# Outputs of the first expert layer turned through memory and VectorE, second layer eight blocks behind, pairs of blocks per step

## The chip, the cores and the metric

The kernel runs on one core of a Trainium2 chip. The metric is the device time of one execution in microseconds (us). The kernel before has a median of 285.72 us over 3 runs (285.41 to 286.38).

## What is computed

`x` is [4, 512, 256], 2048 tokens of 256 features, all in float32. With `xn = layernorm(x)` the result is `x + A(xn) + F(xn)`.

- `A` is a recurrent block: `h = rmsnorm(xn)`; `a = sigmoid(h @ w_a + bias)`, `i = sigmoid(h @ w_i)`, `v = h @ w_v`; a scan over time of `s = a*s + sqrt(1 - a*a)*i*v`; `x1 = xn + s @ out_proj`; then a gated feed-forward with 1024 hidden features: `x1 + (silu(g) * u) @ w_down` with `g, u = split(rmsnorm(x1) @ w_gate_up)`.
- `F` is a mixture of 8 experts, each token in its two best: `y = sum over its 2 experts of p * (relu(xn @ w_fc[e])**2 @ w_proj[e])`, the `p` being the softmax of the two router logits.

## The kernel before

**Precision.** Products are of float32 split into a high part (`_hi`, float32r) and a low rest (`_lo`), three matmuls each: hi*hi, hi*lo, lo*hi. Whatever feeds a matmul must thus be split first: ScalarE copies it to `_hi`, VectorE subtracts to `_lo`.

**Stages.** Up to about 60 us the rows are normalised, the router and the recurrence run, and GpSimd scatters every token's row (and its weight and home row) into `xs_dram`, sorted by expert: 39 blocks of 128 rows, each of one expert. The feed-forward of the recurrent block runs in 32 steps `d` (batch `d // 8`, 128 hidden features `d % 8`): TensorE makes `gate_up(d, 0)` and `gate_up(d, 1)` (six products of 512 columns each, the second in two halves), ScalarE `gate(d)` (silu, L870), VectorE `up(d)` (L1234), ScalarE and VectorE `split_gu(d)` (L890, L1239), and TensorE a step later `down(d - 1)` (twelve products of 256 columns).

**Expert blocks** run inside steps 11 to 24, two or three per step (`THREE`), one more after steps 11 and 17 (`PROJECT`: the output projection of batches 2 and 3, L503) and 13 and 20 (`TURN`: the turn of `h2`, L516). For block i:
- SP loads a pair of blocks from `xs_dram` (L350: for each of 4 groups of 32 columns and each half k, one DMA in pieces of 32 columns, so that what 32 partitions hold are 32x32 tiles); VectorE turns them (`block_turn`, L1304), ScalarE writes `xgT_hi` (`block_in`, L900), VectorE `xgT_lo` (L1311).
- TensorE: first layer `FC` (six products of 256 columns), ScalarE `block_relu` (L922), VectorE `block_square` (L1316) into `act_e`.
- TensorE turns `act_e` by two products with the identity into PSUM bank `T2` (L669); ScalarE `block_middle` writes `aT_hi` (L916), VectorE `aT_lo` (L1320).
- TensorE: second layer `PJ` (six products), ScalarE `block_y` scales by the weight (L909), GpSimd scatters the rows to `y_dram` (L1565).

The order is written out by hand for each engine, and each engine works its list strictly in order, with semaphore waits. TensorE's list has, per block i of a step (v is its place in the step): `expert_in(i)` = PJ of i - 2; for v = 0 `gate_up(d, 0)`, for v = 1 the second half of `gate_up(d, 1)` and half of `down(d - 1)`; `expert_out(i)` = turns of block i - 1, then FC of block i; for v = 0 the first half of `gate_up(d, 1)`, for v = 1 the other half of `down(d - 1)`. VectorE's and ScalarE's lists before are:

```python
# VectorE, block i of step d                 # ScalarE
block_turn(i + 1)                            if v == 0: split_gu(d - 1)
if v == 0: split_gu(d - 1)                   if i >= 2: block_y(i - 2)
if v == 1: up(d)                             if v == 0: gate(d)
if i >= 1: block_middle(i - 1)               if i >= 1: block_middle(i - 1)
block_square(i)                              block_relu(i)
block_in(i + 1)                              block_in(i + 1)
```

`cumulate` and `recur` of batch 3 (scans, L1126, L1131) stand in VectorE's list in steps 14 and 15, after the block's own work, and `take_down` adds a batch's down projection to `Y` (L1262). After the last block SP loads the expert rows back in the tokens' order (`sums`, L402), VectorE adds them in steps 27 to 30 (`add_sum`, L1269), and SP stores the output.

Of the kernel before, what the change touches and what calls it, by code (L numbers as in the profile page):

```python
# [36 lines left out]
def recurrent_moe_block(nc, x, pre_norm_w, w_a, w_i, w_v, out_proj_w, decay_bias, ffn_norm_w,  # L37
# [25 lines left out]
    xs_slot = xs_dram.rearrange("(n p) d -> p n d", p=P)  # L63

# [4 lines left out]
    with ExitStack() as ctx:  # L69
# [129 lines left out]
        xr = [small(f"xr{u}", [P, K, P]) for u in range(2)]  # L199
        xgT = [(small(f"xgT{u}_hi", [P, K, P], F32R), small(f"xgT{u}_lo", [P, K, P], F32R)) for u in range(2)]  # L200
        act_e = [small(f"act_e{u}", [P, D]) for u in range(2)]
        aT = [(small(f"aT{u}_hi", [P, K, P], F32R), small(f"aT{u}_lo", [P, K, P], F32R)) for u in range(2)]
# [3 lines left out]
        xq = [put(f"xq{u}", [P, 2, P // Q, K, Q], F32, X_at + 2 * D * 4 * u) for u in range(XQ)]  # L206
# [37 lines left out]
        xq_loaded, of_slot_loaded = [sem(f"xq_loaded{u}") for u in range(XQ)], [sem(f"of_slot_loaded{h}") for h in range(2)]  # L244
# [3 lines left out]
        t2_done, a_hi, a_split = sem("t2_done"), sem("a_hi"), sem("a_split")  # L248
# [18 lines left out]
        for w, halved in ((w_fc, Wfc), (w_proj, Wpj)):  # L267
            for e in (0, 2, 4, 6):
                pieces.append((w[e:e + 2].rearrange("e (k p) n -> p (e k) n", p=P),
                               [h[:, e:e + 2].rearrange("p e k n -> p (e k) n") for h in halved]))  # L270
        ALL = len(pieces)
# [4 lines left out]
        T2, FC, PJ = 3, 6, 7  # L276
        DOWN = 4

# [8 lines left out]
        LAST = 24  # L287

        THREE = (12, 14, 16, 18, 19, 22, 24)
# [6 lines left out]
        ADD_X = {12: 0, 18: 1, 23: 3}  # L296
# [17 lines left out]

        def stored(i):

            return y_stored[i % YB], 16 * (i // YB + 1)

        def gu_bank(d):
# [5 lines left out]
            return 0 if d <= LAST else 2 * ((d - LAST - 1) % 2)  # L325
# [26 lines left out]
        OF_SLOT = (slice(0, 8), slice(8, 2 * NP))  # L352

        def load_of_slot(eng, part):
            eng.dma_start(of_slot[:, OF_SLOT[part], :],
                          xs_slot[:, OF_SLOT[part], WEIGHT:ROW]).then_inc(of_slot_loaded[part], 16)

        @block.sync
        def _(sp):
# [3 lines left out]
            def load_piece(n):  # L363
                sp.dma_start(pieces[n][1][2], pieces[n][0]).then_inc(w_loaded[n], 16)
# [26 lines left out]
            for n in range(NP):  # L391
                if n >= XQ:
                    sp.wait_ge(turned, 2 * (n - XQ) + 2)
                load_pair(sp, n, range(0 if n else P // Q // 2, P // Q))
                if n == 1:
                    load_of_slot(sp, 1)
# [16 lines left out]
        def _(pe):  # L413
# [111 lines left out]
            def gate_up(d, side, part=None):  # L525

                b, m = divmod(d, M)
                if side == 0 and part in (None, 0):
# [10 lines left out]
                    if d == LAST + 2:  # L539
                        pe.wait_ge(a_split, NB)  # L540
# [37 lines left out]
            def down(d, js=range(J)):  # L578
# [4 lines left out]
                if b == B - 1 and m == 0 and js[-1] == J - 1:  # L583
                    pe.wait_ge(act_ready, NB)
# [72 lines left out]
            sets = [[pe.alloc_register(f"expert{s}_{v}") for v in range(SETS)] for s in range(2)]  # L657
            expert = {}

            def load_experts(i):  # L660
                n = min(SETS, NB - i)
                regs = sets[i // SETS % 2][:n]
# [4 lines left out]
            def block_transpose(bank, src, done):  # L667
                for k in range(K):
                    last = nc.tensor.transpose(ps[:, bank, k * P:(k + 1) * P], src[:, k * P:(k + 1) * P], ident[:, :])  # L669
                last.then_inc(done, 1)  # L670

            def layer(bank, lhs, w, v, done):
# [967 lines left out]
```

## Time and profile before

| what | value |
|---|---|
| median of 3 runs | 285.72 us |
| the profiled execution | 284.51 us |
| its span, first to last instruction | 282.7 us |
| TensorE busy, of the span | 269.5 us (95%) |
| VectorE, ScalarE, GpSimd busy | 206.8, 165.7, 114.3 us |
| granted TensorE clock | 1.00 of full speed (2.4 GHz) |
| share of TensorE in the chain that ended last | 75%, VectorE 12% |

The profile is of one execution. Busy times of TensorE are modelled at their ends (matmuls are pipelined), so the distance from one start to the next says more than a duration. "Idle before" an instruction is what its engine waited, and the arrow names who ended it.

### The profile page before, as it was taken

What the parts mean: (1) busy time and instruction counts of PE and PEld (TensorE: products, weight loads), DVE (VectorE), ACT (ScalarE), POOL (GpSimd) and SP (SyncE); (2) the same over time, 40 slices, a digit from 0 to 9 for tenths busy, and PEclk for the clock granted to TensorE, in tenths of its full rate; (3) what the DMA queues carried; (4) which work ended last, traced back from release to release, by engine and by line L of the source; (5) the groups of instructions that cost most, each with busy time, mean ns of one, the idle gap of its engine ahead of it and who ended that gap; (6) DMA issues with size and microseconds to landing.
All of it is one profiled execution on the core that took longest, in us unless ns stands there. A gap on an engine that the chain in (4) does not pass through costs nothing.

```text
span 282.7 us, 5334 instructions
## 1 busy us (share of the span) xinstructions
PE 269.5 (95%) x1671; PEld 234.6 (83%) x1671; DVE 206.8 (73%) x422; ACT 165.7 (59%) x361; POOL 114.3 (40%) x136
## 2 busy tenths in 40 slices
PE   5989999999999979999999999999999999999995
PEld 5767778888888868988997889888898888888894
DVE  3899999999577998656698966565657565533994
ACT  3798889967486433467746555475775555532231
POOL 6597015888668820046233332155222242250000
PEclk9999999999999999999999999999999999999999
DMA  7999992239202147429424344239434365119962
GB/s 212 352 389 314 293 330 73 94 109 353 99 20 92 60 94 49 61 51 180 82 64 82 68 90 82 47 43 197 84 69 79 67 96 118 37 39 280 381 230 77
DMA packets 75590, 39.15 MB, mean 138 GB/s; under 512 B 50758, under 2 KB 72268, under 8 KB 75564
## 3 DMA queue, kind: packets, MB, share of 16 engines
q1 hardware_dynamic: 67760, 27.10, 38.4%
q0 software_dynamic: 5520, 11.44, 14.1%
q10 hardware_dynamic: 2284, 0.27, 0.7%
q8 instruction: 15, 0.25, 0.3%
q14 instruction: 11, 0.09, 0.1%
HBM read 22.07 MB, written 16.72 MB: 137 GB/s over the span
## 4 chain that ended last, share of the span: by engine, by line
PE 75%; DVE 12%; ACT 4%; DMA 3%; issue 3%; POOL 2%; SPq 0%; ACTq 0%; DVEq 0%; POOLq 0%
PE ps L415 64%; PE ps L503 4%; PE ps L669 3%; DMA sums<-y_dram 2%; PE ps L516 1%; PE ps L419 1%; PE ps L432 1%; ACT h L849 1%; DVE aT_lo L1320 1%; DVE gu L1234 1%; ACT aT_hi L916 1%; DVE guT_lo L1239 1%; DMA y_dram<-yb,home_u 1%; DVE hT_lo L1100 1%; DVE cum L1126 1%
## 5 line engine op out<-in xcount | busy, mean ns | idle before, releaser
L1565 POOL DMA_INDIRECT y_dram<-yb,home_u x39 | 41.3, 1059 | 91.4 <-ACT yb L909 69.7
L1544 POOL DMA_INDIRECT xs_dram<-rows_x,slot_u x32 | 40.5, 1266 | 11.3 <-issue 10.2
L415 PE MATMUL ps<-h2T_lo,Wgu_hi 128*128 128x512 f32 (+1 forms) x132 | 42.4, 386 | 0.0
L415 PE MATMUL ps<-h2T_hi,Wgu_hi 128*128 128x512 f32 (+1 forms) x132 | 41.0, 391 | 0.0
L1320 DVE TENSOR_TENSOR aT_lo<-ps,aT_hi 128x256 fp32r<-128x256 f32 x39 | 16.5, 423 | 32.9 <-ACT aT_hi L916 32.9
L415 PE MATMUL ps<-h2T_hi,Wgu_lo 128*128 128x512 f32 (+1 forms) x132 | 40.4, 387 | 0.0
L415 PE MATMUL ps<-Wd_hi,guT_hi 128*128 128x256 f32 x128 | 36.6, 286 | 1.8 <-DVE Y L1262 1.6
L870 ACT ACTIVATE gu<-ps 128x512 f32<-128x512 f32 x31 | 18.5, 597 | 31.2 <-PE ps L415 31.2
L415 PE MATMUL ps<-Wd_hi,guT_lo 128*128 128x256 f32 x128 | 36.2, 283 | 0.0
L415 PE MATMUL ps<-Wd_lo,guT_hi 128*128 128x256 f32 x128 | 36.1, 282 | 0.0
L1234 DVE TENSOR_TENSOR gu<-gu,ps 128x512 f32<-128x512 f32 x31 | 21.1, 682 | 18.8 <-PE ps L415 18.8
L909 ACT ACTIVATE yb<-ps,of_slot 128x256 f32<-128x256 f32 x39 | 18.5, 474 | 20.4 <-PE ps L415 20.4
L890 ACT ACTIVATE guT_hi<-gu 128x512 fp32r<-128x512 f32 x31 | 19.5, 628 | 15.6 <-DVE gu L1234 13.1
L415 PEld LDWEIGHTS ps<-h2T_lo,Wgu_hi 128*128 128x128 f32 x132 | 24.5, 188 | 4.9
L415 PEld LDWEIGHTS ps<-h2T_hi,Wgu_lo 128*128 128x128 f32 x132 | 24.5, 188 | 4.7
L415 PEld LDWEIGHTS ps<-Wd_hi,guT_hi 128*128 128x128 f32 x128 | 24.1, 189 | 4.2 <-issue 2.0
L916 ACT ACTIVATE aT_hi<-ps 128x256 fp32r<-128x256 f32 x39 | 14.9, 381 | 20.4 <-PE ps L669 20.4
L415 PEld LDWEIGHTS ps<-Wd_lo,guT_hi 128*128 128x128 f32 x128 | 24.1, 189 | 1.1
L415 PEld LDWEIGHTS ps<-Wd_hi,guT_lo 128*128 128x128 f32 x128 | 24.1, 188 | 0.0
L415 PEld LDWEIGHTS ps<-h2T_hi,Wgu_hi 128*128 128x128 f32 x132 | 21.7, 188 | 1.9
L1239 DVE TENSOR_TENSOR guT_lo<-gu,guT_hi 128x512 fp32r<-128x512 f32 x31 | 20.9, 673 | 3.2 <-ACT guT_hi L890 3.0
L415 PE MATMUL ps<-Wpj_hi,aT_hi 128*128 x78 | 17.8, 309 | 3.1 <-DVE aT_lo L1320 3.1
(175 smaller groups left out, 622.2 us busy)
## 6 DMA issues: line engine op xcount, KB each, us to landing
xs_dram<-blank SPq DMA_DIRECT2D x1, 5160.0 KB, 27.1
xq<-xs_dram SPq DMA_DIRECT2D x156, 32.0 KB, 2.1
sums<-y_dram SPq DMA_DIRECT2D x8, 512.0 KB, 7.7
Wgu_raw<-in_L_attn_w_gate_up_dram SPq DMA_DIRECT2D x4, 512.0 KB, 8.7
Wfc_raw<-in_L_ffn_w_fc_dram SPq DMA_DIRECT2D x4, 512.0 KB, 10.2
Wpj_raw<-in_L_ffn_w_proj_dram SPq DMA_DIRECT2D x4, 512.0 KB, 6.2
rows_x<-in_L_attn_x_dram SPq DMA_DIRECT2D x3, 512.0 KB, 6.6
rows_x<-in_L_attn_x_dram POOLq DMA_DIRECT2D x3, 512.0 KB, 6.1
```

Of the source, the lines that this page charges most:

```text
L415: return nc.tensor.matmul(dst, lhs, rhs, start=start, stop=stop, skip_group_check=group)
L503: last = nc.tensor.matmul(ps[:, aside(b) + side, (j % 2) * D:(j % 2 + 1) * D], dec[b][:, k, j * P:(j + 1) * P], Wo[:, k, :], start=k == 0, ...
L669: last = nc.tensor.transpose(ps[:, bank, k * P:(k + 1) * P], src[:, k * P:(k + 1) * P], ident[:, :])
L870: A.activation(gu[d % 2][:, :], ps[:, gu_bank(d), :], ACT.Silu).then_inc(sg_ready, 1)
L890: A.activation(guT[d % 2][0][:, :], gu[d % 2][:, :], ACT.Copy).then_inc(gu_hi, 1)
L909: A.activation(yb[i % YB][:, :], ps[:, PJ, 0:D], ACT.Copy, scale=of_slot[:, i, 0:1]).then_inc(y_ready, 1)
L916: A.activation(aT[i % 2][0][:, :, :].rearrange(flat), ps[:, T2, 0:D], ACT.Copy).then_inc(a_hi, 1)
L1234: V.tensor_tensor(gu[d % 2][:, :], gu[d % 2][:, :], ps[:, gu_bank(d) + 1, :], ALU.mult).then_inc(gu_ready, 1)
L1239: V.tensor_tensor(guT[d % 2][1][:, :], gu[d % 2][:, :], guT[d % 2][0][:, :].bitcast(F32), ALU.subtract).then_inc(gu_split, 1)
L1320: V.tensor_tensor(aT[i % 2][1][:, :, :].rearrange(flat), ps[:, T2, 0:D], aT[i % 2][0][:, :, :].rearrange(flat).bitcast(F32), ALU.subtract) ...
L1544: pool.indirect_dma_start(out=xs_dram, in_=rows_x[:, b, j, :], in_offset=None, out_offset=bass.IndirectOffsetOnAxis(ap=slot_u[:, n:n + 1], ...
L1565: pool.indirect_dma_start(out=y_dram, in_=yb[i % YB][:, :], in_offset=None, out_offset=bass.IndirectOffsetOnAxis(ap=home_u[:, i:i + 1], ax ...
```

## The change

- First-layer outputs are no longer turned by TensorE. SP stores the pair's `act_e` to a new `act_dram` (two DMAs), loads it back in 32-column pieces (four DMAs into `aq`, one per 32 partitions), and VectorE turns it per block (`act_turn`) into `aT_raw`, which lies at the place of `aT_lo`. `block_middle` then reads SBUF and not PSUM.
- The second layer of block i - 8 (`LAG`) runs in front of block i. The first layer ends with step 23 (`LAST`), the last eight second layers run four per step in 24 and 25 (`DRAIN`). `FC` and `PJ` have two PSUM banks each.
- `block_turn`, `block_in`, `block_relu`, `block_square` work on pairs (512 columns), each in every second block.
- The token rows are loaded in pieces of 64 columns, four DMAs a pair for eight; for that `w_fc`'s rows are loaded in another order (16 DMAs for 4). The weights and homes of the slots come in one DMA.
- In VectorE's list the `take_down`s of batch 0 stand in front of `cumulate(2, 1)`.

The core of the diff (comment-free; "..." marks what is left out):

```diff
+    act_dram = nc.dram_tensor("act_dram", [NP, K, 2 * P, P], F32, kind="Internal").ap()
+    act_pair = act_dram.rearrange("n k (a i) c -> n i (k a) c", i=Q)
...
-        LAST = 24
-        THREE = (12, 14, 16, 18, 19, 22, 24)
+        LAST = 23
+        DRAIN = 25
+        LAG = 8
+        THREE = (12, 14, 15, 16, 18, 19, 21, 22, 23)
...
         def load_pair(eng, n, groups):
             for r in groups:
-                mine = xq[n % XQ][r * Q:(r + 1) * Q].rearrange("i v g k c -> i (v g) k c")
-                for k in range(K):
-                    col = k * P + r * Q
-                    eng.dma_start(mine[:, :, k, :], xs_pair[n, :, :, col:col + Q]).then_inc(xq_loaded[n % XQ], 16)
+                eng.dma_start(xq[n % XQ][r * Q:(r + 1) * Q].rearrange("i a k c -> i a (k c)"),
+                              xs_pair[n, :, :, r * K * Q:(r + 1) * K * Q]).then_inc(xq_loaded[n % XQ], 16)
...
+            def store_act(n):
+                sp.wait_ge(act_ready, n + 1)
+                for v in range(2):
+                    sp.dma_start(act_dram[n, :, v * P:(v + 1) * P, :].rearrange("k p c -> p k c"),
+                                 act_e[n % 2][:, v, :].rearrange("p (k c) -> p k c", c=P)).then_inc(act_stored[n % 2], 16)
+
+            def load_act(n):
+                if n >= 2:
+                    sp.wait_ge(a_turned, 2 * n - 2)
+                else:
+                    sp.wait_ge(o_done, 6)
+                sp.wait_ge(act_stored[n % 2], 32 * (n // 2 + 1))
+                for r in range(P // Q):
+                    sp.dma_start(aq[n % 2][r * Q:(r + 1) * Q].rearrange("i k v g c -> i (k v g) c"),
+                                 act_pair[n, :, :, r * Q:(r + 1) * Q]).then_inc(aq_loaded[n % 2], 16)
...
-            for n in range(NP):
-                if n >= XQ:
-                    sp.wait_ge(turned, 2 * (n - XQ) + 2)
-                load_pair(sp, n, range(0 if n else P // Q // 2, P // Q))
+            for n in range(NP + 4):
+                if n < NP:
+                    if n >= XQ:
+                        sp.wait_ge(turned, n - XQ + 1)
+                    load_pair(sp, n, range(0 if n else P // Q // 2, P // Q))
...
+                if n >= 4:
+                    load_act(n - 4)
+                if 3 <= n < NP + 3:
+                    store_act(n - 3)
...
             # TensorE
+            def expert_out(i):
+                if i >= 0:
...
+                    pe.wait_ge(a_split, i + 1)
+                    if i >= 2:
+                        pe.wait_ge(y_ready, i - 1)
+                    layer(PJ[i % 2], 0, aT[i % 2], slice(0, P), Wpj, expert[i], pj_done)
...
+                    for v, i in enumerate(blocks_of(d)):
+                        expert_out(i - LAG)
                         if v == 0:
                             gate_up(d, 0, 0)
                             gate_up(d, 0, 1)
                         if v == 1:
                             gate_up(d, 1, 1)
                             down(d - 1, range(0, 2))
-                        expert_out(i)
+                        expert_in(i)
                         if v == 0:
                             gate_up(d, 1, 0)
                         if v == 1:
                             down(d - 1, range(2, 4))
+                elif d <= DRAIN:
+                    d0, d1, d2, d3 = drained_by(d)
+                    expert_out(d0)
+                    gate_up(d, 0)
+                    expert_out(d1)
+                    gate_up(d, 1)
+                    expert_out(d2)
+                    down(d - 1)
+                    expert_out(d3)
...
             # ScalarE
                     for v, i in enumerate(blocks_of(d)):
+                        block_y(i - LAG - 1)
                         if v == 0:
                             split_gu(d - 1)
...
                             gate(d)
...
+                        if i % 2 == 0:
+                            block_relu(i // 2 - 1)
+                        block_middle(i - LAG + 1)
+                        if i % 2 == 1:
+                            block_in(i // 2 + 1)
...
             # VectorE
+            def act_turn(i):
+                if 0 <= i < NB:
+                    n, v = divmod(i, 2)
+                    dve.wait_ge(aq_loaded[n % 2], 16 * (P // Q) * (n // 2 + 1))
                     if i >= 2:
+                        dve.wait_ge(pj_done, i - 1)
+                    V.transpose(aT[i % 2][2][:, :, :].rearrange("p k (g s) -> p k g s", s=Q),
+                                aq[n % 2][:, :, v, :, :]).then_inc(a_turned, 1)
...
-            cumulate(2, 1)
             take_down(0, 0)
             take_down(0, 1)
+            cumulate(2, 1)
...
                     for v, i in enumerate(blocks_of(d)):
-                        block_turn(i + 1)
+                        act_turn(i - LAG + 1)
...
                         if v == 1:
                             up(d)
-                        if i >= 1:
-                            block_middle(i - 1)
-                        block_square(i)
-                        block_in(i + 1)
+                        if i % 2 == 0:
+                            block_turn(i // 2 + 1)
+                        else:
+                            block_in(i // 2 + 1)
+                        if i % 2 == 0:
+                            block_square(i // 2 - 1)
+                        block_middle(i - LAG + 1)
...
                 if d in PROJECT or d in TURN:
                     i = block_after(d)
+                    act_turn(i - LAG + 1)
                     if d in PROJECT:
                         add_residual(PROJECT[d], 0)
                     if d in TURN:
                         split_h2(TURN[d], range(0, 1))
-                    block_square(i)
-                    block_in(i + 1)
+                    if i % 2 == 0:
+                        block_turn(i // 2 + 1)
+                    else:
+                        block_in(i // 2 + 1)
+                    if i % 2 == 0:
+                        block_square(i // 2 - 1)
+                    block_middle(i - LAG + 1)
                     if d in TURN:
                         split_h2(TURN[d], range(1, 2))
```

## Rows read from the trace of the kernel before

**Rows 1.** Busy time, clock and DMA in the stretch of the expert blocks.
```profile
core 0: us, PE busy (x) PEld busy (x) DVE busy (x) ACT busy (x) POOL busy (x), PEclk, DMA share, GB/s
109.46:251.92 142.46, 139.07 (x949) 125.34 (x950) 93.94 (x214) 82.29 (x213) 47.51 (x46) 1.00 0.44 81
```

**Rows 2.** Waits: who waited for whom: us in total, times, longest.
```profile
PE ps L415 <- DVE aT_lo L1320: 3.1, 7, 0.4
...
PE ps L415 <- DVE Y L1262: 1.6, 1, 1.6
```

**Rows 3.** Pieces of the chain that ended last: start us, us, what.
```profile
139.31 0.44 PE ps L516 x4
...
176.12 1.73 PE ps L503 x8
177.85 0.22 PE ps L669 x2
```

**Rows 4.** Timeline of step 19: start us, us, engine line op out<-in.
```profile
190.19 0.48 PE L415 MATMUL ps<-Wpj_hi,aT_hi 128*128 x2 [0.43 <-DVE aT_lo L1320]
...
190.99 0.62 PE L415 MATMUL ps<-h2T_hi,Wgu_hi 128*128 128x512 f32 x2
...
192.37 0.38 PE L669 MATMUL ps<-ident,act_e 128*128 128x128 f32 x2
...
192.57 0.60 ACT L870 ACTIVATE gu<-ps 128x512 f32<-128x512 f32 x1 [0.91 <-PE ps L415]
...
193.06 0.38 ACT L916 ACTIVATE aT_hi<-ps 128x256 fp32r<-128x256 f32 x1
...
193.47 0.42 DVE L1320 TENSOR_TENSOR aT_lo<-ps,aT_hi 128x256 fp32r<-128x256 f32 x1 [1.57 <-ACT aT_hi L916]
...
194.03 0.48 PE L415 MATMUL ps<-Wpj_hi,aT_hi 128*128 x2
...
195.79 0.69 DVE L1234 TENSOR_TENSOR gu<-gu,ps 128x512 f32<-128x512 f32 x1 [0.74 <-PE ps L415]
...
196.23 0.38 PE L669 MATMUL ps<-ident,act_e 128*128 128x128 f32 x2
...
197.16 0.28 PE L415 MATMUL ps<-Wd_hi,guT_hi 128*128 128x256 f32 x1
```

**Rows 5.** Timeline where the first expert block starts.
```profile
106.83 1.22 DVE L1229 TENSOR_TENSOR Wpj_lo<-Wpj_raw,Wpj_hi 128x1024 fp32r<-128x1024 f32 x1
...
107.97 0.44 DVE L1304 STREAM_TRANSPOSE xr<-xq 128x256 f32<-128x256 f32 x1
...
108.44 0.42 ACT L900 ACTIVATE xgT_hi<-xr 128x256 fp32r<-128x256 f32 x1 [2.55 <-DVE xr L1304]
...
108.76 0.61 ACT L890 ACTIVATE guT_hi<-gu 128x512 fp32r<-128x512 f32 x1
108.89 0.43 DVE L1311 TENSOR_TENSOR xgT_lo<-xr,xgT_hi 128x256 fp32r<-128x256 f32 x1 [0.48 <-ACT xgT_hi L900]
...
109.46 0.51 PE L415 MATMUL ps<-Wfc_hi,xgT_hi 128*128 x2 [0.50 <-DVE xgT_lo L1311]
```

**Rows 6.** Timeline: start of step 14, last second layer, steps 26 to 28.
```profile
139.61 0.48 PE L415 MATMUL ps<-Wpj_hi,aT_hi 128*128 x2
...
250.49 0.28 PE L415 MATMUL ps<-Wd_hi,guT_hi 128*128 128x256 f32 x1
...
251.92 0.62 PE L415 MATMUL ps<-h2T_hi,Wgu_hi 128*128 128x512 f32 x2
...
261.35 1.23 DVE L1269 TENSOR_TENSOR Y<-Y,sums 128x1024 f32<-128x1024 f32 x1 [1.51 <-DMA sums<-y_dram]
...
263.36 0.39 PE L415 MATMUL ps<-Wd_hi,guT_hi 128*128 128x256 f32 x1
```

**Rows 7.** The tile `xq`: its loads by SP (issue, ns min/median/max) and landing.
```profile
L350 SPq DMA_DIRECT2D xq<-xs_dram x156: 302/451/1271, 102.8 to 233.5; - x156
...
DMA to landing us min/median/max: 1.7/2.1/4.7
```

More of the change, by code:

```diff
@@ L198, in recurrent_moe_block, with turned_halves @@
         over = [moe_at]
[L199 to L202, printed above, removed]
+        def turned_halves(name, n):
+            hi = small(name + "_hi", [P, K, n * P], F32R)
+            at = over[0]
+            return hi, small(name + "_lo", [P, K, n * P], F32R), put(name + "_raw", [P, K, n * P], F32, at)
+        xgT = [turned_halves(f"xgT{u}", 2) for u in range(2)]
+        aT = [turned_halves(f"aT{u}", 1) for u in range(2)]
         yb = [small(f"yb{u}", [P, D]) for u in range(YB)]
@@ L313, in recurrent_moe_block, with drained_by @@
         assert blocks_of(LAST)[-1] == NB - 1
+        def drained_by(d):
+            return range(NB - LAG + 4 * (d - LAST - 1), NB - LAG + 4 * (d - LAST))
+        assert drained_by(DRAIN)[-1] == NB - 1
         def stored(i):
@@ L656, in _ @@
             pe.wait_ge(experts_ready, 1)
-            sets = [[pe.alloc_register(f"expert{s}_{v}") for v in range(SETS)] for s in range(2)]
+            sets = [[pe.alloc_register(f"expert{s}_{v}") for v in range(SETS)] for s in range(4)]
             expert = {}
@@ L665, in load_experts, with layer @@
                     expert[i + v] = pe.snap(reg, min_val=0, max_val=E - 1)
[L667 to L672, printed above, removed]
+            def layer(bank, half, lhs, cols, w, v, done):
                 for n, (l, h) in enumerate(PRODUCTS):
                     for k in range(K):
-                        last = product(ps[:, bank, 0:D], lhs[l][:, k, :], w[h][:, v, k, :],
+                        last = product(ps[:, bank, half * D:(half + 1) * D], lhs[l][:, k, cols], w[h][:, v, k, :],
                                        n + k == 0, n == 2 and k == K - 1)
@@ new lines, in expert_in @@
+                if i % SETS == 0:
+                    load_experts(i)
+                if v == 0:
+                    pe.wait_ge(xg_split, n + 1)
+                    if n >= 2:
+                        pe.wait_ge(act_ready, n - 1)
+                    if n == 0:
+                        pe.wait_ge(we_lo, FFN_ALL + 4 - 3)
+                    if n == 1:
+                        pe.wait_ge(gu_ready, FIRST)
+                layer(FC[n % 2], v, xgT[n % 2], slice(v * P, (v + 1) * P), Wfc, expert[i], fc_done)
@@ L1284, in add_down, with homes @@
                                     ALU.add).then_inc(out_ready, 1)
-            def homes(part):
-                dve.wait_ge(of_slot_loaded[part], 16)
-                mine = OF_SLOT[part]
-                at = of_slot[:, mine, 1]
-                chain.step(V.scalar_tensor_tensor(out=no_home[:, mine], in0=at, scalar=0.0, in1=no_home[:, mine],
+            def homes():
+                dve.wait_ge(of_slot_loaded, 16)
+                at = of_slot[:, :, 1]
+                chain.step(V.scalar_tensor_tensor(out=no_home[:, :], in0=at, scalar=0.0, in1=no_home[:, :],
@@ L1606, in _ @@
                         add_x(ADD_X[d])
-                if (d in PROJECT or d in TURN) and block_after(d) >= 3:
-                    scatter(block_after(d) - 3)
-            for i in range(NB - 3, NB):
+                if (d in PROJECT or d in TURN) and block_after(d) > LAG:
+                    scatter(block_after(d) - LAG - 1)
+            for i in range(NB - LAG - 1, NB):
                 scatter(i)
```

273 lines of the change are left out of this document (135 added, 138 removed).

## The prediction

> **What bounds the kernel now.** I read the windows view first, over the stretch in which the expert blocks run: from the first product of block 0 to the start of step 26 the span has 142.46 us, TensorE (PE) is busy in 139.07 of them, VectorE in 93.94, ScalarE in 82.29, the granted clock is 1.00 of full speed (2.4 GHz) and the DMA engines are busy 0.44 of the time [rows 1]. So PE sets the pace here, and a change pays only in what PE does or waits for. The waits view then says who PE waits for: 1.6 us once for a sum of the down projection (`Y` L1262), and 3.1 us in 7 waits for `aT_lo`, the low half of the turned outputs that the second layer eats [rows 2]. The idle time is counted against modelled ends; by start times each of the 7 costs 0.6. The pieces of the chain give PE's unit prices: 0.22 us for the two turns of a block, 1.73 for half a projection, 0.44 for half an h2 turn [rows 3].
>
> The third reading is one step in the timeline [rows 4], d = 19, since all that follows is built from it. From the start of a second-layer product at 190.19 it takes 0.80 to the first gate product, 1.38 for six products of 512 columns (to 192.37), and 0.93 for the two turns with a first-layer product (196.23 to 197.16), so a layer's six products of 256 columns take 0.71. ScalarE starts `gate` 2.38 after the start of the block, the next instruction 0.49 later (it starts 0.11 before the end of a 0.60 one); VectorE's `aT_lo` takes 0.42, and PE starts 0.14 after it, at 194.03: 3.84 after 190.19, of which PE's own work is 3.8. The present order is thus already at the limit: gate, aT_hi, aT_lo, next block. In the next block `up` starts 1.76 after PE's start.
>
> **The change, part by part.**
> Removed: 39 pairs of turns, 39 x 0.22 = 8.6 us, and the 7 waits of 0.6 = 4.2 us, since they come from a turn that is followed at once by the product that needs it. A layer that comes after 512-column products takes 0.80 and not 0.71, which stays in the own times below. VectorE, which turns the outputs instead, needs 0.44 for 256 columns [rows 5] where PE needs 0.22, but has room. The Trainium skill, "VectorE: DVE Perf Modes" (Rules for kernel authors), speaks against the swap: a full 128x128 turn belongs on TensorE where the result may go to PSUM, as it may here. By that rule the swap would cost up to 39 x (0.44 - 0.22) = 8.6 us where the rows alone give 8.6 us back; the sum below takes the rows, since VectorE has room for the 17 us.
>
> Own time of PE, per block, afterwards. First block of a step (v0): 0.80 + 1.38 + 0.79 + 0.69 = 3.66. Second (v1): 0.80 + 0.69 + 3 x 0.71 = 3.62. Third (v2): 0.80 + 0.71 = 1.51.
>
> Added: the order in which `aT_lo` is made. PE begins block i with the second layer of i - 8, whose `aT_lo` is made by VectorE at the end of its list for block i - 1, behind everything else of that list: the turn of a pair or its `xgT_lo`, and the square of a pair. ScalarE has `block_relu` in front of its `aT_hi`, and `block_in` right behind. These are on 512 columns now: ScalarE 0.60 from PSUM, 0.62 from SBUF (L890), VectorE 0.69 (next one 0.61 later; 0.08 before the end, as 106.83 + 1.22 and 107.97 show) [rows 4, 5]. A turn of 512 columns is in no row; 256 take 0.44, as near to the 0.42 of a plain one as makes 0.71 for 512 likely, and 0.88 (twice) is the upper end.
> - v0, i odd: VectorE must wait for `xgT_hi`, that for gate. 2.38 + 0.49 (aT_hi starts) + 0.31 (xgT_hi starts) + 0.62 + 0.03 + 0.61 (xgT_lo) + 0.42 (aT_lo) + 0.14 = 5.00.
> - v0, i even: gate, relu, square, aT_lo: 2.38 + 0.49 + 0.60 + 0.03 + 0.61 + 0.42 + 0.14 = 4.67.
> - v1, i even: up, turn of a pair, square, aT_lo: 1.76 + 0.61 + 0.63 + 0.61 + 0.42 + 0.14 = 4.17. i odd: 1.76 + 0.61 + 0.61 + 0.42 + 0.14 = 3.54, under PE's own 3.62.
> - v2, i odd: VectorE begins its list as PE begins (0.21 before): turn to 0.22, aT_hi 0.25, xgT_hi 0.56 to 1.18, xgT_lo 1.21, aT_lo 1.82 to 2.24, PE at 2.38. i even (VectorE is 0.1 further ahead): 0.06 + 0.63 + 0.61 + 0.42 + 0.14 = 1.86.
>
> Both layers run in steps 14 to 23: five steps of either parity, four of each with a v2 (14, 16, 18, 22 odd; 15, 19, 21, 23 even). 5 x 5.00 + 5 x 4.67 + 5 x 4.17 + 5 x 3.62 + 4 x 2.38 + 4 x 1.86 = 104.3. The projection's block in d = 17: own 0.80 + 1.73 + 0.79 + 1.73 = 5.05, by VectorE's list 5.2. The turn's block in d = 20: 1.23 to the end of the h2 turn, ScalarE 0.2 + 0.7, VectorE 0.67 + 0.6 + 0.42 + 0.14 gives 4.0, against 2.47 of own work. The scans of batch 3 (14, 15) stand between `aT_lo` of one block and the turn of the next; about 1.8 us each; three have cover in VectorE's wait for gate or up, the fourth (recur in v1 of 15, before a v2) has none: 2.0, with 0.3 for the others. Steps 24 and 25, four second layers each: 4 x 0.71 + 3 x 0.08 + 2.76 + 1.42 = 7.26 of own work, all else covered. Sum from d = 14 to step 26: 104.3 + 5.2 + 4.0 + 2.3 + 14.5 = 130.3. Now it takes 251.92 - 139.61 = 112.3 [rows 6], but second layers of eight blocks have moved in.
>
> Before d = 14: the swap of `take_down` with `cumulate` lifts PE's 1.6 us wait, but block 0 is due to VectorE, whose list up to 106.83 is the same minus 0.5 of waiting for PE. Then the pair costs 0.27 more to turn, 0.2 on ScalarE, 0.26 on VectorE, so the first product starts at 109.67 for 109.46 [rows 5]: the 1.6 turns into a wait there. Without second layers d = 11 takes 1.5 + 2.9 + 4.2 = 8.6, d = 12 6.5, d = 13 5.8 and its turn block 4.6 (h2T_lo stands before `aT_lo` of block 1, with the pair's turn and square between; own work 2.5). d = 14 starts at 109.67 + 25.5 = 135.1, and step 26 at 265.4 for 251.92: 13.5 later.
>
> The end: the last second layer now ends where step 26 starts, today 1.43 before it (250.49, 251.92). From its end to the first add of the sums are 10.86 us, from that to PE's restart 2.01 [rows 6]: 12.87 after step 26's start for 11.44 now, 1.4 more. After it VectorE's adds have the same cover.
>
> DMA: a pair took 8 loads in 128-byte pieces; it takes 4 of 256, 2 stores, and 4 loads of 128. SP's issue takes 0.45, landing 1.7 to 4.7, 2.1 in the middle [rows 7]. A pair's load of outputs is let go by the turn three blocks before it is needed, 11.5 us: 4 x 0.45 + 4.7 = 6.5 fits. The store has six. I cost them at nothing; the 12 further issues for `w_fc` (5.4 us of SP) end long before use. y scatters, one per block as now, stay.
>
> Sum: +13.5 + 1.4 = +14.9 us. The profiled execution took 284.51 (span 282.7), so 299.4; it is 1.2 under the median of 285.72, on which scale I give **300.5 us**.
>
> **Rivals.**
> 1. PE is not held, as the change means it: the lists of VectorE and ScalarE keep ahead of the second layer. Then the same counts with own times alone give 8.6 + 6.5 + 8.2 + 92.4 + 14.5 = 130.2, step 26 at 239.9, and with the end +1.4: 10.6 us less, **275.1**. For it speaks the load: VectorE has 49 us to spare in 142 [rows 1]. Against it, a load is no order: gate cannot start before 2.38. It decides where PE's waits for `aT_lo` in 31 blocks are under 10.6 us together instead of the 25.5 that I count (0.35 a block, not 0.8). Chance 0.13.
> 2. The trip through memory is late. Its price: a load slower than the three blocks of cover holds the turn, each us over costs one in every four blocks or so; 2 us over make some 16: **316**. Against it: the loads of now, in the same 128-byte pieces, land in 2.1 us [rows 7]; for it, that there are more of them beside the scatters. Chance 0.06. The Trainium skill, "DMA: Bandwidth & Descriptors" (Specifications), wants at least 512 bytes a transfer for the full rate, and has the engines read, modify and write below that; by this rule the new loads are the ones to be late.
> 3. Part of the waits holds, and they just eat the gain: 285.7. Chance 0.03.
> 4. Mine: 0.78. Its own range, from 0.1 us a block either way (3 us) and a turn of 0.88 (1.6 more): 296 to 306.
>
> **Range and chances.** 289 to 309 takes mine in with room to either side for a partial hold and a slightly late load. About 0.3% is what a measurement of this kernel can tell from no change. Slower 0.82 (mine, 2 and the slower half of what lies between), same 0.03, faster 0.15 (rival 1 and a little of the partial hold).
>
> **What would show it.** In the waits view PE for VectorE `aT_lo` rises from 7 waits to over 20, 15 us or more; the windows view has PE's busy time in the stretch down by about 8 and the stretch longer; VectorE waits for `xgT_hi` once per odd v0; first block at 109.7; no wait for `Y` L1262; the aq loads land within 5 us and nobody waits for them; the add of the sums starts 10.9 after the last layer. I am wrong if PE's second layers follow each other at 3.7, 3.6, 1.5 us in steps 14 to 23, or if `act_turn` is seen waiting for DMA.

## The result and the profile after

The changed kernel takes **304.5 us** (median of 4 runs, 304.4 to 304.66) where the kernel before, on the same chip, takes 286.05 (4 runs, 285.41 to 286.74): a ratio of 1.0645, 95% interval 1.0617 to 1.0673. It is slower, and by about what was forecast (300.5, range 289 to 309).

The page of the changed kernel, cut to the busy times, the slices of PE and its clock, the chain's shares, and of part 5 the groups whose idle time grew:

```profile
PE 266.6 (88%) x1593; PEld 229.4 (76%) x1593; DVE 213.2 (70%) x402; ACT 159.4 (53%) x323; POOL 112.4 (37%) x136
...
PE   5999999999999969968885889789869789899795
...
PEclk9999999999999999998999999999999999999799
...
PE 50%; DVE 23%; issue 10%; ACT 6%; DMA 6%; SPq 3%; POOL 2%; ACTq 0%; DVEq 0%; POOLq 0%
...
L458 PE MATMUL ps<-Wpj_hi,aT_hi 128*128 x78 | 18.3, 315 | 23.4 <-DVE aT_lo L1383 23.4
...
L1358 DVE TENSOR_TENSOR xgT_lo<-xgT_raw,xgT_hi 128x512 fp32r<-128x512 f32 x20 | 13.8, 690 | 21.8 <-ACT xgT_hi L930 21.7
```

PE's share of the chain fell from 75% to 50%, VectorE's rose from 12% to 23%. PE no longer sets the pace there: its second layers (`Wpj_hi,aT_hi`) wait 23.4 us for `aT_lo`, and VectorE itself stands 21.7 us waiting for ScalarE's `xgT_hi`. The waits view of the changed kernel (us in total, times, longest), which answers to [rows 2]:

```profile
PE ps L458 <- DVE aT_lo L1383: 23.4, 28, 2.1
...
DVE xgT_lo L1358 <- ACT xgT_hi L930: 21.7, 13, 4.0
...
DVE aT_raw L1376 <- DMA aq<-act_dram: 3.1, 2, 2.3
```

Seven waits have become 28, and 3.1 us have become 23.4. The wait for `Y` has gone. The windows view, which answers to [rows 1]: before step 14, steps 14 to 25, the rest (columns as there):

```profile
109.52:135.47 25.95, 23.36 (x150) 21.14 (x151) 17.35 (x32) 13.00 (x31) 3.23 (x4) 1.00 0.72 117
135.47:268.36 132.89, 111.90 (x721) 98.14 (x722) 82.90 (x163) 62.02 (x143) 40.74 (x42) 0.99 0.64 141
268.36:302.80 34.44, 29.04 (x170) 25.52 (x168) 19.11 (x26) 8.13 (x15) 2.52 (x3) 0.95 0.65 206
```

From step 14 to step 26 PE is busy 111.90 us of 132.89: 21 us of idling. One v0 block with i odd (d = 16) shows how it comes about, in the timeline of all engines:

```profile
160.98 0.43 DVE L1376 STREAM_TRANSPOSE aT_raw<-aq 128x256 f32<-128x256 f32 x1
...
161.19 0.48 PE L458 MATMUL ps<-Wpj_hi,aT_hi 128*128 x2 [2.08 <-DVE aT_lo L1383]
...
163.55 0.60 ACT L902 ACTIVATE gu<-ps 128x512 f32<-128x512 f32 x1 [2.71 <-PE ps L458]
164.05 0.41 ACT L950 ACTIVATE aT_hi<-aT_raw 128x256 fp32r<-128x256 f32 x1
164.35 0.62 ACT L930 ACTIVATE xgT_hi<-xgT_raw 128x512 fp32r<-128x512 f32 x1
...
165.01 0.69 DVE L1358 TENSOR_TENSOR xgT_lo<-xgT_raw,xgT_hi 128x512 fp32r<-128x512 f32 x1 [3.02 <-ACT xgT_hi L930]
...
165.62 0.45 DVE L1383 TENSOR_TENSOR aT_lo<-aT_raw,aT_hi 128x256 fp32r<-128x256 f32 x1
...
166.20 0.48 PE L458 MATMUL ps<-Wpj_hi,aT_hi 128*128 x2 [1.27 <-DVE aT_lo L1383]
```

The `aT` of a block needs nothing of the step in which it is made: VectorE began the turn of its input at 160.98, before the step. Still ScalarE makes `aT_hi` after `gate`, since `gate` stands ahead of it in its list, and VectorE makes `aT_lo` after `xgT_lo`, which waits for ScalarE. Hence 5.01 us from PE's start to the next (161.19 to 166.20), for 3.66 of PE's own work.

### The profile page after: what moved, and what is told of

Same layout as the page of the kernel before. It is cut to its first block, busy times and chain, and to the rows that moved or that the text cites. A ratio compares the mean times of both kernels' runs of the same rounds, so it can differ in the third digit from the quotient of the medians.

```text
span 302.8 us, 5115 instructions
## 1 busy us (share of the span) xinstructions
PE 266.6 (88%) x1593; PEld 229.4 (76%) x1593; DVE 213.2 (70%) x402; ACT 159.4 (53%) x323; POOL 112.4 (37%) x136
## 4 chain that ended last, share of the span: by engine, by line
PE 50%; DVE 23%; issue 10%; ACT 6%; DMA 6%; SPq 3%; POOL 2%; ACTq 0%; DVEq 0%; POOLq 0%
PE ps L458 42%; PE ps L546 4%; DVE aT_lo L1383 4%; DMA sums<-y_dram 3%; ACT xgT_hi L930 2%; DVE act_e L1367 2%; SPq L401 2%; DVE xgT_raw L1351 2%; DVE gu L1284 2%; DVE cum L1176 2%; DVE xgT_lo L1358 2%; DMA act_dram<-act_e 2%; DVE aT_raw L1376 1%; ACT act_e L941 1%; PE ps L475 1%
## 5 line engine op out<-in xcount | busy, mean ns | idle before, releaser
L1645 POOL DMA_INDIRECT y_dram<-yb,home_u x39 | 38.4, 984 | 94.5 <-ACT yb L960 93.0
L902 ACT ACTIVATE gu<-ps 128x512 f32<-128x512 f32 x31 | 18.5, 597 | 58.5 <-PE ps L458 56.5
L1624 POOL DMA_INDIRECT xs_dram<-rows_x,slot_u x32 | 41.5, 1297 | 11.3 <-issue 10.2
L458 PE MATMUL ps<-h2T_hi,Wgu_hi 128*128 128x512 f32 (+1 forms) x132 | 41.8, 398 | 0.0
L458 PE MATMUL ps<-Wpj_hi,aT_hi 128*128 x78 | 18.3, 315 | 23.4 <-DVE aT_lo L1383 23.4
L458 PEld LDWEIGHTS ps<-Wpj_hi,aT_hi 128*128 128x128 f32 x78 | 12.2, 189 | 31.7 <-issue 31.4
L950 ACT ACTIVATE aT_hi<-aT_raw 128x256 fp32r<-128x256 f32 x39 | 16.2, 417 | 29.8 <-DVE aT_raw L1376 29.5
L1358 DVE TENSOR_TENSOR xgT_lo<-xgT_raw,xgT_hi 128x512 fp32r<-128x512 f32 x20 | 13.8, 690 | 21.8 <-ACT xgT_hi L930 21.7
```

The lines of the kernel that those rows point to most:

```text
L458: return nc.tensor.matmul(dst, lhs, rhs, start=start, stop=stop, skip_group_check=group)
L902: A.activation(gu[d % 2][:, :], ps[:, gu_bank(d), :], ACT.Silu).then_inc(sg_ready, 1)
L950: A.activation(aT[i % 2][0][:, :, :], aT[i % 2][2][:, :, :], ACT.Copy).then_inc(a_hi, 1)
L1358: V.tensor_tensor(xgT[n % 2][1][:, :, :], xgT[n % 2][2][:, :, :], xgT[n % 2][0][:, :, :].bitcast(F32), ALU.subtract).then_inc(xg_split, 1)
L1624: pool.indirect_dma_start(out=xs_dram, in_=rows_x[:, b, j, :], in_offset=None, out_offset=bass.IndirectOffsetOnAxis(ap=slot_u[:, n:n + 1], ...
L1645: pool.indirect_dma_start(out=y_dram, in_=yb[i % YB][:, :], in_offset=None, out_offset=bass.IndirectOffsetOnAxis(ap=home_u[:, i:i + 1], ax ...
```

## The experiments

The kernel before took 285.7 to 285.8 us beside all of them. Every edit is to the changed kernel unless it says otherwise.

**The lists' order: one half, the other half, both.** `block_middle` (it makes `aT_hi` on ScalarE, `aT_lo` on VectorE) goes to where its input is ready. ScalarE's part:

```diff
                         if v == 0:
                             split_gu(d - 1)
+                        block_middle(i - LAG + 1)
+                        if v == 0:
                             gate(d)
                         if i % 2 == 0:
                             block_relu(i // 2 - 1)
-                        block_middle(i - LAG + 1)
```

VectorE's part:

```diff
                         if v == 0 and d > FIRST and d % M == 1:
                             take_down(d // M - 1, 1)
+                        block_middle(i - LAG + 1)
                         if v == 1:
                             up(d)
...
                         if i % 2 == 0:
                             block_square(i // 2 - 1)
-                        block_middle(i - LAG + 1)
```

In the lists of the `PROJECT` and `TURN` blocks it goes to the front in the same way. In steps 24 and 25 nothing is moved.

Both parts:

> The changed kernel with aT_hi and aT_lo made first in every block: ScalarE's block_middle in front of gate and block_relu, VectorE's in front of up, block_turn, block_in and block_square. Nothing else moves, the same work is done. Theory (order of the lists): v0, v1 and v2 of steps 14 to 23 fall from 5.0/4.7, 4.1/3.6 and 2.4/1.8 us to TensorE's own 3.7, 3.6 and 1.5; the waits for aT_lo (23.4 us in 28) fall under 4; the time from 304.5 to 281, between 277 and 285. Rival (trip through memory is late): the transfers are the same, so over 298. Rival (instructions on 512 columns make VectorE's list too long, in whatever order): over 293.

Measured: 287.8 us (10 runs, 285.31 to 289.93), ratio to before 1.0057 [1.0029, 1.0085]. VectorE's part alone (one run each here and next):

> Only VectorE's list reordered; ScalarE still makes aT_hi behind gate and relu. Theory: v1 and v2 are freed, v0 stays held by ScalarE: odd 2.38 + 0.49 + 0.41 + 0.03 + 0.42 + 0.14 = 3.9, even 0.5 more = 4.4; 285 to 291. If VectorE's place of aT_lo is not the cause: 300 or more.

289.02 us. ScalarE's part alone:

> Only ScalarE's list reordered; aT_lo stays last in VectorE's. Theory: VectorE still waits for xgT_hi or relu behind gate, so v0 odd gains only the 0.3 of aT_hi, the others nothing: 301 to 304. If ScalarE's place of aT_hi were the cause it would come near the run with both: under 290.

302.1 us. So 16.7 of the 18.5 us lost come back by an edit that changes no work at all, and most of it with VectorE's part alone: this order was the cause. The steps of the version with both parts, as starts of its second layers in the timeline of PE, for v0, v1, v2 of step 21 from 208.04 on:

```profile
208.04 0.48 PE L458 MATMUL ps<-Wpj_hi,aT_hi 128*128 x2
...
211.66 0.40 PE L458 MATMUL ps<-Wpj_hi,aT_hi 128*128 x2
...
215.20 0.40 PE L458 MATMUL ps<-Wpj_hi,aT_hi 128*128 x2
...
216.62 0.40 PE L458 MATMUL ps<-Wpj_hi,aT_hi 128*128 x2
```

3.62, 3.54 and 1.42 us: PE's own time, as the prediction's first rival had it (3.66, 3.62, 1.51). But I had expected 281, and waits for `aT_lo` under 4 us, and that missed by 7. The waits and the landing of its `aq` loads (the profiled execution took 289.93 us, the longest of the ten):

```profile
PE ps L458 <- DVE aT_lo L1384: 10.0, 10, 2.0
...
DVE aT_raw L1377 <- DMA aq<-act_dram: 6.2, 4, 2.3
...
DMA to landing us min/median/max: 1.8/2.2/3.6
```

Of PE's 10.0 us, 4.5 fall between 142.90 and 158.44, in steps 14 to 16, where the scans of batch 3 stand in VectorE's list. Besides, with PE faster, 6.2 us of waits for the trip through memory appear, though a load lands as fast as ever (2.2). The timeline of SP, which issues every one of these DMAs in this version, shows how little room it has in step 21:

```profile
208.77 1.01 SPq L391 DMA_DIRECT2D act_dram<-act_e  x2
209.82 2.02 SPq L371 DMA_DIRECT2D xq<-xs_dram  x4
211.95 2.17 SPq L401 DMA_DIRECT2D aq<-act_dram  x4
214.16 1.00 SPq L391 DMA_DIRECT2D act_dram<-act_e  x2
215.21 2.05 SPq L371 DMA_DIRECT2D xq<-xs_dram  x4
217.36 2.65 SPq L401 DMA_DIRECT2D aq<-act_dram  x4
```

SP issues without a pause here: 10 DMAs take 5.4 us (208.77 to 214.16), and a pair of blocks now takes PE some 5.7. A delay in that list is hardly made up again. The turns that wait come later: at 225.10, 241.43, 246.58 and 251.47, three of the four in steps 24 and 25, which begin at 235.13. There SP no longer issues all the time. The pieces of the chain that ended last (SPq L391 is a store, L401 a load):

```profile
232.78 0.49 SPq L391
...
233.32 3.90 DMA act_dram<-act_e
...
237.28 0.32 SPq L401
...
239.24 0.49 SPq L391
...
239.77 2.62 DMA act_dram<-act_e
...
242.46 0.32 SPq L401
```

The chain is on SP and its DMAs alone from 217.75 to 251.44: four loads, the store behind them, the landing of that store, the next four loads. In SP's list the store of a pair stands in front of that pair's loads, which wait for it to land, and once the token rows are loaded nothing is left to issue between the two; by its waits view SP stands still 12.0 us, in 6 waits, for stores to land. A round takes 5.2 us (237.28 to 242.46), where steps 24 and 25 have 3.6 us of work for PE per pair. The store itself goes out late: VectorE begins the last square at 237.72, and SP issues the store of that pair at 244.42.

**Stores issued by GpSimd.** The version with both parts, and the two stores of `act_e` per pair taken out of SP's list and issued by GpSimd, in its list behind a block's scatter:

```diff
-                if 3 <= n < NP + 3:
-                    store_act(n - 3)
...
+                    if i % 2 == 0 and i:
+                        store_act(i // 2 - 1)
```

> The run with aT_hi and aT_lo first, with the stores of act_e issued by GpSimd in place of SP, so SP has 8 issues a pair, not 10. Theory: act_turn's waits for its loads (6.2 us) go, and the 3 to 5 us behind them; 282 to 286 for 287.8. If SP is not the cause: the waits stay, 287 to 288.

Measured: **280.92 us** (4 runs, 280.47 to 282.51), ratio 0.9856 [0.9819, 0.9892]: 6.9 us less than without, a little less than the 282 to 286 expected, and now 1.4% faster than the kernel before. VectorE's waits for `aq` fall to 1.9 us in 3, PE's for `aT_lo` to 6.3 in 7, and the mean clock of the profiled execution is 1.00 where it was 0.98. The edit does two things: SP issues 8 DMAs a pair for 10, and a store no longer stands behind SP's loads. The last square begins at 231.69 here and its store is issued at 232.91, 1.2 us later and not 6.7. No run tells what each of the two is worth. The same edit without the order of the lists turned:

> The changed kernel with the stores of act_e issued by GpSimd in place of SP, the list of each block in its old order. Theory (in the changed kernel TensorE waits on VectorE's aT_lo, which stands at the list's end; the DMA path is late only in steps 24 and 25, 3.1 us): 301 to 304.5 us. Rival, that the issuing queue is the main cause of the loss: under 295 us.

303.08 us (one run): 1.4 less than the changed kernel, and PE still waits 22.1 us in 26 for `aT_lo`. SP's list was thus not what held the changed kernel; it shows only once the lists of VectorE and ScalarE let PE run. The Trainium skill, "DMA: Bandwidth & Descriptors" (Rules for kernel authors), says that spreading DMAs over the issuing engines brings no bandwidth and only saves the issuing engine's time. The runs agree on the landing, which stays at 2.2 to 2.5 us for the `aq` loads; the issuing engine's time that is saved is 1.0 of SP's 5.4 us per pair. But here the order of SP's list counts beside it, as the late stores show.

**More load on the trip.** Three ways to put more on SP and on the DMA engines. First, each load of `aT` preceded by a copy of the same 128-byte pieces from DRAM to DRAM, which VectorE waits for too:

```diff
                 for r in range(P // Q):
+                    sp.dma_start(junk_dram[n, r * Q:(r + 1) * Q, :].rearrange("i (a c) -> i a c", c=Q),
+                                 act_pair[n, :, :, r * Q:(r + 1) * Q]).then_inc(aq_loaded[n % 2], 16)
```

> The changed kernel; in front of each load of a pair's outputs SP copies the same 128-byte pieces once more, to a memory of their own, and act_turn waits for both: twice the loads' DMAs and bytes in the trip. Theory (trip hidden): the same within 1 us in steps 14 to 23, at most 3 us more in steps 24 and 25, where two turns already waited 3.1 us for their loads. Rival (trip late): 10 us more or above.

329.59 us (one run), 25 more than the changed kernel: a miss by far. Next, four DMAs of 128 bytes each, DRAM to DRAM, that nothing waits for before the end:

```diff
+                for r in range(P // Q):
+                    sp.dma_start(junk_dram[n, r:r + 1, :], act_dram[n, 0, r:r + 1, 0:Q]).then_inc(junk_done, 16)
```

> The changed kernel; in front of each load of a pair's outputs SP issues four DMAs of 128 bytes each, which nobody waits for until the end: the number of issues of the run with doubled loads, without their bytes and without a longer trip. Theory (SP's issue time, 0.49 us each, was what the doubled loads ran out of: 14 issues are 7 us of a pair's 7): 10 us or more over 304.5. Rival (the bytes or the landing of the trip): within 3 us of 304.5.

370.75 us (one run), 66 more. The same number of issues, but into on-chip memory, tells the number of issues from the transfers inside DRAM:

```diff
+                if n >= 2:
+                    sp.wait_ge(spare_loaded[n % 2], 64 * (n // 2))
+                for r in range(P // Q):
+                    sp.dma_start(spare[n % 2][r * Q:(r + 1) * Q, :],
+                                 act_dram[n, 0, r * Q:(r + 1) * Q, 0:Q]).then_inc(spare_loaded[n % 2], 16)
```

> The changed kernel with four more small loads per pair, each of 32 pieces of 128 bytes from act_dram into a spare tile of on-chip memory, issued by SP ahead of the loads of aT; nothing but SP waits for them, two pairs later. Theory that SP's issuing is what is short (10 issues a pair now, 14 then, at about 0.49 us each: 6.9 us of a pair of about 7.2 us): the loads of aT come late as in e4_double_loads, 314 us or more. Rival, that the two runs before were slow through the transfers between places of DRAM themselves: within 5 us of the changed kernel, 304 to 309 us.

316.02 us (one run), 11.5 more, as the theory of SP's issuing has it, with landings of 2.2 us as before. Where they fall, in its windows view, from step 14 to the last block of step 23, and from there to step 26:

```profile
137.00:253.79 116.79, 95.81 (x613) 83.83 (x614) 72.16 (x139) 52.45 (x121) 33.08 (x34) 0.99 0.66 144
253.79:281.13 27.34, 20.67 (x111) 18.12 (x110) 11.32 (x25) 9.57 (x23) 7.63 (x8) 0.81 0.44 102
```

In the first stretch the 14 issues of a pair take 7.1 us in SP's timeline and a pair of blocks on the average 7.5 (104.3 us for 28 blocks, as the prediction summed them), so little is lost: 116.8 us, 115.4 in the changed kernel. In the second a pair of second layers has only 3.6 us of work, a round of SP takes 7 (258.56 to 265.61), the landing of the store included, and there it takes 27.3 us for 17.5, at a mean clock of 0.81.

The run with doubled loads fits the same account. Its copies take 0.63 us each to issue, so that the 14 issues of a pair take 8.0 us (209.04 to 217.07 in SP's timeline) and are too long for the 7.5 of the first stretch too. The stores still land in 2.2 us and GpSimd's scatters in 2.9; the landing of the copies and of the loads behind them cannot be told apart in the trace, so a part of the 25 us may be theirs.

In the run with tiny copies from DRAM to DRAM the issue count is the same, and yet the landing itself is slow. Its DMA issues (last column us to landing; 2.2, 2.2 and 2.8 for these three in the changed kernel):

```profile
act_dram<-act_e SPq DMA_DIRECT2D x40, 128.0 KB, 3.6
aq<-act_dram SPq DMA_DIRECT2D x80, 64.0 KB, 4.5
...
y_dram<-yb,home_u POOLq DMA_INDIRECT x39, 5.6
```

So the number of issues accounts for 11.5 of the 66 us, and perhaps for up to the 25 of the doubled loads, since an issue takes 0.59 us here and not 0.42. Beyond that, these copies go with slower landings of the other DMAs, GpSimd's scatters too, and SP takes 2.1, 3.6 and 3.0 us to issue the two stores of a pair (from 199.81 on) for 1.0. It is not that pieces of 128 bytes are written to DRAM: the doubled loads write 40960 of them, 5.2 MB, and leave the stores at 2.2 us and the scatters at 2.9. The tiny copies write even smaller ones: their trace has 1280 packets of 8 bytes more than that of the changed kernel, 16 for each copy of 128 bytes. The Trainium skill, "DMA: Bandwidth & Descriptors" (Specifications), has the engines read, modify and write below 512 bytes. That holds for both runs alike, so by itself it does not account for the difference; what does, no run here shows.

**The swap of `take_down` with `cumulate`**, alone, in the kernel before:

```diff
-            cumulate(2, 1)
             take_down(0, 0)
             take_down(0, 1)
+            cumulate(2, 1)
```

> The kernel before with one edit of the change, the take_downs of batch 0 in front of cumulate(2, 1) in VectorE's list. Theory: TensorE's wait of 1.6 us for Y goes, and comes back in front of block 0, whose inputs VectorE delivers no more than 0.5 us earlier: the ratio between 0.998 and 1.000. Rival (the 1.6 us are kept): 0.994.

285.97 us (10 runs, 284.54 to 288.24), ratio 1.0005 [0.9988, 1.0022]. The 1.6 us wait for `Y` is gone and PE waits 3.2 for `xgT_lo` of block 0 in its place, as the prediction said (it is 2.6 in the changed kernel; the profiled execution here was the longest of the ten).

**What the turns on TensorE are worth**, in the kernel before. They are left out: `aT` is made from whatever bank `T2` holds, so the experts' outputs are not computed.

```diff
-                    block_transpose(T2, act_e[(i - 1) % 2], t2_done)
+                    pe.sem_inc(t2_done, 1)
```

> The kernel before with TensorE's turns of the activations left out: aT is made from whatever the PSUM bank holds, so the experts' outputs are not computed. It prices what the change takes off TensorE. If the turns cost their 8.6 us of busy time and most of the 0.6 us waits on act_e stay: 274 to 278 us. If they cost 275 ns each or more, as single ones do: 272 or less. If they lie in idle time that stays: 282 or more.

281.5 us (one run), only 4.3 less than before, and by the spans 3.0 (279.7 for 282.7): between the expectations, nearest the one that the turns lie in time that stays idle. PE's busy time falls by 5.3 (264.2 for 269.5) and not by 8.6; as its ends are modelled, the starts say more. Step 19 in PE's timeline, and the two starts of the kernel before that [rows 4] lacks:

```profile
188.97 0.47 PE L415 MATMUL ps<-Wpj_hi,aT_hi 128*128 x2 [0.46 <-DVE aT_lo L1320]
...
192.81 0.47 PE L415 MATMUL ps<-Wpj_hi,aT_hi 128*128 x2
...
196.42 0.40 PE L415 MATMUL ps<-Wpj_hi,aT_hi 128*128 x2
...
198.67 0.53 PE L415 MATMUL ps<-Wpj_hi,aT_hi 128*128 x2 [0.47 <-DVE aT_lo L1320]
```

```profile
197.87 0.40 PE L415 MATMUL ps<-Wpj_hi,aT_hi 128*128 x2
...
200.12 0.47 PE L415 MATMUL ps<-Wpj_hi,aT_hi 128*128 x2 [0.43 <-DVE aT_lo L1320]
```

The v0 still takes 3.84 us, as before [rows 4], since there the chain from `gate` to `aT_lo` sets the pace; the v2 takes 2.25, as it did too. Only the v1 has become shorter, 3.61 for 3.84. In the order before, a turn pays in one block of each step, 14 times 0.23 = 3.2 us. PE's 7 waits for `aT_lo` stay (3.3 us for 3.1).

**Towards a better version.** The version with both lists turned and stores by GpSimd, and besides: `cumulate` and `recur` of batch 3 one per step (14 to 17) and not two; the turn of the first pair ahead of `up(10)`, and two of the pieces of `Wpj_lo` made behind blocks 1 and 3; the last second layer ahead of `down(24)`; `split_gu` ahead of `add_sum` on VectorE.

```diff
-                        if d in (14, 15) and v == 0:
-                            cumulate(3, d - 14)
-                        if (d, v) in ((14, 2), (15, 1)):
-                            recur(3, d - 14)
+                        if (d, v) in ((14, 0), (16, 0)):
+                            cumulate(3, (d - 14) // 2)
+                        if (d, v) in ((15, 0), (17, 0)):
+                            recur(3, (d - 15) // 2)
...
                         up(d)
+                        split_gu(d)
                         if 0 <= b < B:
                             add_sum(0, b)
-                        split_gu(d)
-                        if 0 <= b < B:
                             add_sum(1, b)
```

> That, and: the scans of batch 3 one per step in steps 14 to 17; the last low halves of w_proj made behind block 0's inputs, block_turn(0) in front of up(10); the last second layer in front of down(24); split_gu in front of both adds of the sums. Theory: 2 us at the start, 3 at the scans, 1.4 + 1.7 at the end, 2 or 3 of half clock that went with these waits: 274 to 280, faster than both kernels.

279.27 us (4 runs, 277.92 to 280.3), ratio 0.9763 [0.9731, 0.9796]. Then with the last of these edits for the first sum only (the diff is against that version):

```diff
                         up(d)
+                        if 0 < b < B:
+                            add_sum(0, b)
                         split_gu(d)
-                        if 0 <= b < B:
+                        if b == 0:
                             add_sum(0, b)
+                        if 0 <= b < B:
                             add_sum(1, b)
```

> The version of e9_all (both halves' list order turned, stores issued by GpSimd, scans one per step, the turn of a block ahead of the second layer's step 10), but with the second layer's step put ahead of the add of the sums only for the first sum; the later ones as in the kernel before. If the three stalls of 0.65, 0.68 and 0.43 us in the last half steps of e9_all come from that displacement, 277 to 279.5 us; if they come from the tail's own chain (a half's aT_lo waits for its own first layer), no change from 279.3.

**279.02 us** (4 runs, 277.01 to 279.91), ratio 0.9747 [0.9692, 0.9802]: the fastest of the study by its median, though not to be told from the one before it. Its span is 277.5 us (278.3 there) and the three stalls in the last half steps are gone. Its windows, before step 14, steps 14 to 23, 24 and 25, and the rest:

```profile
109.38:133.69 24.31, 24.31 (x151) 22.26 (x151) 17.48 (x30) 10.84 (x28) 6.99 (x9) 0.93 0.64 108
133.69:231.35 97.66, 92.22 (x628) 84.21 (x626) 75.62 (x144) 55.77 (x128) 58.30 (x64) 1.00 0.76 172
231.35:247.07 15.72, 14.87 (x99) 13.05 (x97) 10.03 (x23) 8.86 (x21) 11.72 (x14) 1.00 0.61 160
247.07:277.50 30.43, 27.27 (x170) 24.27 (x168) 18.99 (x25) 7.66 (x14) 1.91 (x2) 0.99 0.73 229
```

PE is busy 92.22 us of 97.66 in steps 14 to 23, where the changed kernel took 116.9 for the same steps (135.47 to 252.33).

## Why the prediction held, and where it was off

- **The mechanism** was right: the order of the lists, not the load on the engines. Blocks in steps 14 to 23, by the starts of PE, against the prediction: v0 with i odd 5.01 (161.19 to 166.20) for 5.00; v0 even 4.66 (148.64 to 153.30) for 4.67; v1 even 4.10 for 4.17; v1 odd 3.62 for 3.62; v2 odd 2.42 for 2.38; v2 even 1.75 for 1.86. The projection's block took 5.28 for 5.2, the turn's block in d = 20 4.09 for 4.0. The version with both lists turned is the counter-proof.
- **The terms before step 14** held: first product at 109.52 for 109.67, step 14 at 135.47 for 135.1. The wait for `Y` turned into one in front of block 0, as the swap alone confirms.
- **A turn of 512 columns** on VectorE took 0.70 us (0.67 to 0.71), the lower of the two ends.
- **The sum was 4.0 us short** on the scale of medians, 5.2 on that of the profiled span (302.8 for 282.7 + 14.9 = 297.6). Steps 14 to 23 took 1.1 more than the 115.8 of the sum, and more than that is one stretch at half clock: v0 of step 14 took 6.57 us for 5.0. Steps 24 and 25 took 16.0 for 14.5 (252.33 to 268.36). The tail took 34.44 for 32.2: the first add of the sums came 11.53 after step 26's start for 10.86, PE's restart 13.53 for 12.87, and half clock followed it (0.58 and 0.56 from 282 to 286). With 0.4 before step 14 that is the 5.2. The sum had no term for half clock.
- **The step that was off** is "I cost them at nothing" of the DMAs, and in it "6.5 fits": it weighed the loads of one pair against 11.5 us of cover, and neither what SP issues in all against the time of a pair nor that these loads wait until the store that stands in front of them has landed. In steps 24 and 25, with pairs every 3.6 us, the chain runs over SP's loads and two such landings of 2.21 and 2.50 us (254.71 and 259.61), and two turns waited 3.1 us for their loads. The prediction had named a wait of `act_turn` for a DMA as a sign that it is wrong; the sign came, but at the size of those 3.1 us beside the 23.4 that PE waits for `aT_lo`. The rival of a late trip named slow loads as its cause, and those never came: `aq` loads landed in 2.2 us, 4.1 at most. By the rule cited for that rival from the Trainium skill, "DMA: Bandwidth & Descriptors" (Specifications), the loads in 128-byte pieces would be the ones to be late; the trace of the changed kernel does not show it.
- **"39 x 0.22 = 8.6 us, and the 7 waits of 0.6"** as the price of what is removed was too high for the order before: there the turns are worth 4.3 us, as the v0 and the v2 are set by ScalarE's and VectorE's chain to `aT_lo`, and the 7 waits do not come from the turns, since they stay without them. For the order with the second layer eight behind no run puts the turns back; that its blocks take 3.62, 3.54 and 1.42 us without them is PE's own time, as the sum had it. The forecast that PE's busy time in the stretch would fall by about 8 did not come true in the changed kernel, 135.26 us (23.36 + 111.90) for 139.07; in the best version it is 131.40, 7.7 less.
- **In the working itself** the last lines do not quite add up. 14.9 us more than 285.72 is 300.6. The 3 us either way and the 1.6 give 297.5 to 305.1, not 296 to 306. And the chances of the forecast and of rival 2, 0.78 and 0.06, are already more than the 0.82 for slower. None of it changes the answer.
- **Rival 1** (275.1) is nearly reached once more than the two lists is mended: 287.8 with the lists alone, 279.0 in the best version. Steps 14 to 25 took 113.4 us there (133.69 to 247.07), the rival had 106.9; PE's waits for `aT_lo` that are left, 5.2 us in 8, are most of the difference.

**Still open:** why the tiny copies inside DRAM slow the others; how much of the 6.9 us is SP's issue time and how much the place of the stores in its list; what decides whether a wait of PE is followed by half clock; and which of the four further edits brought the last 2 us.

## What to carry to other kernels

When a stage is moved many blocks away from its producer, its place in every engine's list must move as well: an instruction that is ready early but stands behind one that waits is as late as that one. Here the place of one call in VectorE's list was worth 15 us. Then count what each queue issues per unit of work against the time that the unit is to take, in every stage: at 0.5 us an issue, ten a pair leave next to no slack at 5.7 us a pair. The queue's list is such a list too: a load that waits for a store to land holds up all that is behind it. And the busy time of an instruction is not its price: measure by leaving it out.

## What the runs showed of the hardware that was not expected

**The clock after a wait.** The granted clock of TensorE halved (0.5 of full speed, 1.2 GHz) after some waits and not after others of the same length. In the changed kernel PE waited 2.05 us ahead of step 14 and ran at a mean of 0.51 in the window right behind; the wait of 2.58 us ahead of block 0 left it at 1.00:

```profile
109.51 0.51 PE L458 MATMUL ps<-Wfc_hi,xgT_hi 128*128 x2 [2.58 <-DVE xgT_lo L1358]
...
135.47 0.68 PE L458 MATMUL ps<-Wpj_hi,aT_hi 128*128 x2 [2.05 <-DVE aT_lo L1383]
...
109.00:111.00 2.00, 1.49 (x9) 1.39 (x10) 2.00 (x3) 0.65 (x2) 0.00 (x0) 1.00 0.73 129
...
135.50:138.00 2.50, 2.50 (x9) 2.30 (x10) 1.32 (x3) 0.00 (x0) 0.70 (x1) 0.51 0.75 152
```

The version with both lists turned has the same wait ahead of block 0 (2.60) and the clock at 0.50 from 111 to 113; with the stores on GpSimd the wait is 2.61 and the clock 1.00. A new wait can thus cost more than its length: the first six products of step 14 took 1.33 us and the next six 2.40, for 0.8 and 1.38.

**Issuing.** An issue by SP hardly depends on the size: 0.49 us in the middle for 64 KB into on-chip memory, 0.42 for 4 KB; 0.63 for 64 KB inside DRAM, 0.59 for 128 bytes.
